# Attention block on one core: plain queries made with dimensions on the partitions, one small query transfer a step, rows of x interleaved

## What is computed

```
xn = _layernorm(x)
c_Q = rms_norm(xn @ Wq_down, q_norm_w)                 # 192 wide
q_nop = (c_Q @ Wq_up)     # 16 heads x 128             plain part of a query
q_pe = rope(c_Q @ Wq_pe)  # 16 heads x 64              rotated part
c_KV = rms_norm(xn @ Wkv_down, kv_norm_w)              # 128 wide
k_nop, v = split(c_KV @ Wkv_up)  # 8 key heads x 128 each
k_pe = rope(rms_norm(xn @ Wk_pe, k_pe_norm_w))         # 64 wide, shared by the heads
scores = ([q_nop, q_pe] . [k_nop, k_pe]) * SCALE, causal mask, softmax -> attn
y = attn @ v ; x + y @ Wo + ternary(xn) @ w_rram.T
```

## Time and profile before

| what | value |
|---|---|
| time, median of 3 runs | 1701.72 us (1698.91 to 1708.31) |
| the profiled execution's own time | 1702.12 us |
| its span, first to last instruction | 1700.3 us |
| PE busy | 1633.8 us (96%), 9612 matmuls |
| DVE / ACT / POOL busy | 77% / 65% / 34% |
| mean DMA rate | 150 GB/s |

### The profile page before, as it was taken

The page is one execution under the profiler, slowest core; times in us unless marked ns, Lnnn a source line. Parts: engine busy times, 40 slices in busy tenths (PEclk is TensorE's granted clock), DMA queues, the critical chain, the costliest instruction groups (busy, mean ns, idle before and its releaser), DMA issues.

```text
span 1700.3 us, 30407 instructions
## 1 busy us (share of the span) xinstructions
PE 1633.8 (96%) x9612; PEld 837.1 (49%) x9612; DVE 1301.6 (77%) x3369; ACT 1104.3 (65%) x2464; POOL 580.3 (34%) x1048
## 2 busy tenths in 40 slices
PE   4789999999999999999999999999999999999999
PEld 3445455544544445545454445554455444555444
DVE  5888878768688687777868787876868868777765
ACT  5877667567576666656666566756756666666663
POOL 3323334333343233433333333433333323333320
PEclk9999999999999999999999999999999999999999
DMA  9467988879979889987969988887987988998886
GB/s 259 97 103 141 150 147 154 147 134 158 152 138 161 145 152 159 166 149 122 161 126 167 170 148 147 154 149 129 161 153 141 159 144 151 162 159 147 147 153 126
DMA packets 914889, 254.58 MB, mean 150 GB/s; under 512 B 901608, under 2 KB 904042, under 8 KB 914410
## 3 DMA queue, kind: packets, MB, share of 16 engines
q1 hardware_dynamic: 904032, 228.98, 80.3%
q10 hardware_dynamic: 9162, 17.37, 3.3%
q0 software_dynamic: 1536, 6.29, 1.1%
HBM read 19.76 MB, written 8.39 MB: 17 GB/s over the span
## 4 chain that ended last, share of the span: by engine, by line
PE 71%; DMA 9%; issue 6%; ACT 5%; DVE 5%; SPq 2%; POOL 2%; ACTq 0%; DVEq 0%; POOLq 0%
DMA FT<-F 6%; PE bank L695 5%; PE bank L693 5%; PE bank L692 5%; PE bank L694 5%; PE bank L795 5%; PE bank L794 5%; PE bank L793 5%; PE bank L737 4%; PE bank L738 4%; PE bank L739 4%; PE bank L705 4%; ACT P L1082 2%; SPq L1848 2%; DVE F L1499 2%
## 5 line engine op out<-in xcount | busy, mean ns | idle before, releaser
L1082 ACT ACTIVATE P<-P,nm 128x256 f32<-128x256 f32 (+15 forms) x512 | 381.7, 746 | 439.6 <-DVE nm L1485 439.6
L1485 DVE CUSTOM_DVE_ANT_0 P<-bank,mask,neg 128x256 f32<-128x256 f32 (+15 forms) x512 | 383.0, 783 | 270.0 <-PE bank L705 261.8
L1719 POOL TENSOR_SCALAR sn<-sm 128x1 f32<-128x1 f32 x512 | 209.0, 409 | 926.1 <-ACT P L1082 918.6
L1077 ACT ACTIVATE F<-P,rc 128x256 f16<-128x256 f32 (+15 forms) x512 | 366.7, 743 | 101.0 <-DVE rc L1493 62.4
L1499 DVE SCALAR_TENSOR_TENSOR F<-P,rc,F 128x256 f16<-128x256 f32 (+15 forms) x512 | 401.6, 796 | 2.7 <-ACT F L1077 2.3
L692 PE MATMUL bank<-K,Q 128*128 128x512 f16 (+7 forms) x760 | 241.7, 319 | 0.8 <-DMA Q<-QS 0.8
L695 PE MATMUL bank<-K,Q 128*128 128x512 f16 (+7 forms) x760 | 241.7, 319 | 0.0
L693 PE MATMUL bank<-K,Q 128*128 128x512 f16 (+7 forms) x760 | 241.7, 319 | 0.0
L694 PE MATMUL bank<-K,Q 128*128 128x512 f16 (+7 forms) x760 | 241.7, 319 | 0.0
L793 PE MATMUL bank<-WO,YH 128*128 128x512 f16 x512 | 194.3, 379 | 4.0 <-DVE YL L1505 3.7
L794 PE MATMUL bank<-WO,YH 128*128 128x512 f16 x512 | 194.0, 379 | 0.0
(11 more groups left out here) (229 smaller groups left out, 2874.8 us busy)
## 6 DMA issues: line engine op xcount, KB each, us to landing
out<-X ACTq DMA_DIRECT2D x31, 256.0 KB, 3.6
X<-in_x ACTq DMA_DIRECT2D x28, 256.0 KB, 3.5
FT<-F SPq DMA_TRANSPOSE x348, 4.4
wo<-in_Wo POOLq DMA_DIRECT2D x4, 1024.0 KB, 7.0
Q<-QS SPq DMA_TRANSPOSE x256, 3.6
V<-CC SPq DMA_DIRECT2D x32, 64.0 KB, 3.0
X<-in_x SPq DMA_DIRECT2D x4, 256.0 KB, 8.4
kv<-in_Wkv_up POOLq DMA_DIRECT2D x1, 1024.0 KB, 12.5
```

Of the source, the lines that this page charges most:

```text
L1077: return e.eng.activation(dst, src, ACT.Copy, scale=scale)
L1082: e.eng.activation(m.P[:, u % 4, 0:w], m.P[:, u % 4, 0:w], ACT.Exp, bias=m.nm[:, u % 8:u % 8 + 1], scale=-1.0, accum_out=m.sm[:, u % 8:u % ...
L1485: e.eng.tensor_tensor_reduce(out=m.P[:, u % 4, 0:w], in0=m.pS[u % 2][:, off:off + w], in1=m.mask[:, end - w:end], scale=m.neg[:, :], scala ...
```

## The change

1. **Rows of x.** `rows` gives a tile's 128 rows in another order: partition 2k + a holds row 64a + k, so the two sides alternate from partition to partition. x is loaded and the output stored in that order; the table for the rotation is loaded likewise, by two transfers. V is brought back to natural order by two transfers with every second partition of CC. K is turned into a new buffer KT, and GpSimd copies it in natural order to its place (`keep_keys`, new semaphore `k_at`).
2. **Plain queries.** `up` now takes slices of WM as weights and C as the moving operand. Its output has the 128 dimensions on the partitions and 128 positions on the columns, one head after another: 4 heads x 5 matmuls of 128 columns. ScalarE and VectorE write high and low parts straight into Q, which has four buffers in place of two.
3. **Rotated part.** Only this is turned: one transfer of 128 positions x 512 columns a step, from QS to QP.
4. **Weights of the score products.** The 128 queries of a side are now every second column (`[:, a::2]`) of two neighbouring heads.
5. **Output of the value products.** The pattern into pY becomes `p (h q a) -> p a h q`: each side writes every second 4-byte word, so that the positions in pY come to lie in the new order.
6. **Half matmuls.** The four 64-row halves of `up` stand between the matmuls of `diagonal_half`.

```
 def rows(dram, t):
     b, i = ORDER[t]
-    return dram[b, i * 128:i * 128 + 128, :]
+    return by_places(dram[b, i * 128:i * 128 + 128, :])
+def by_places(dram):
+    return dram.rearrange("(a k) n -> k a n", a=2)
...
 def query_weights(m, n, h):
     a, g = divmod(h, 2)
-    Q = m.Q[:, n % 2, a, :]
-    return [Q[:, 256 * x + 128 * g:256 * x + 128 * g + 128] for x in range(3)]
+    Q, heads = m.Q[:, n % 4, :, :], slice(2 * g, 2 * g + 2)
+    return [x[:, heads, :].rearrange("p h q -> p (h q)")[:, a::2] for x in (Q[:, 0:4, :], Q[:, 4:8, :], m.QP[:, n % 2, :, :])]
...
     def up(self, n, begun=False):
-        e.eng.matmul(m.pU, hq, W[:, WMA:WMA + 512], start=not begun, stop=False)
-        if not begun:
-            e.eng.matmul(m.pU, lb, W[:, WMB:WMB + 512], start=False, stop=False)
-        e.eng.matmul(m.pU, hq, W[:, WMA + 512:WMA + 1024], start=False, stop=False)
-        e.eng.matmul(m.pU, lq, W[:, WMA:WMA + 512], start=False, stop=False)
-        e.eng.matmul(m.pU, hb, W[:, WMB:WMB + 512], start=False, stop=True).then_inc(s.up, 1)
+        for h in range(4):
+            o, W = m.pU[:, 128 * h:128 * h + 128], m.WM[:, g, 128 * h:]
+            e.eng.matmul(o, W[:, WMA:WMA + 128], hq, start=not begun and h == 0, stop=False)
+            if not begun:
+                e.eng.matmul(o, W[:, WMB:WMB + 128], lb, start=False, stop=False)
+            e.eng.matmul(o, W[:, WMA + 512:WMA + 640], hq, start=False, stop=False)
+            e.eng.matmul(o, W[:, WMA:WMA + 128], lq, start=False, stop=False)
+            op = e.eng.matmul(o, W[:, WMB:WMB + 128], hb, start=False, stop=(h == 3))
+        op.then_inc(s.up, 1)
...
     def weighed(n, j, lo, hi):
-        o = m.pY[n % 2].rearrange("p (h a q) -> p a h q", h=4, a=2)[:, lo // 2:hi // 2]
+        o = m.pY[n % 2].rearrange("p (h q a) -> p a h q", h=4, a=2)[:, lo // 2:hi // 2]
...
+    def keep_keys(self, t):
+        e.wait_ge(s.k_in, 16 * (t + 1))
...
+        e.eng.tensor_copy(m.K[:, :, at:at + 128].rearrange("p c (a k) -> p c a k", a=2),
+                          m.KT.rearrange("p c (k a) -> p c a k", a=2)).then_inc(s.k_at, 1)
...
     def turn_queries(n):
-        e.wait_ge(s.qh, n + 1)
-        e.wait_ge(s.ql, n + 1)
         e.wait_ge(s.ph, n + 1)
         e.wait_ge(s.pl, n + 1)
         if n >= 2:
             e.wait_ge(s.s, 4 * (n - 1))
-        for a in range(2):
-            e.eng.dma_start_transpose(out=m.Q[:, n % 2, a, :].rearrange("p (c q) -> p c q", q=64),
-                                      in_=m.QS[64 * a:64 * a + 64, n % 2, :]).then_inc(s.q_in[a][n % 2], 16)
+        e.eng.dma_start_transpose(out=m.QP[:, n % 2, :, :], in_=m.QS[:, n % 2, :]).then_inc(s.q_in[n % 2], 16)
```

More of the change, by code:

```diff
@@ L225, in __init__ @@
         self.K = own("K", [128, 4, 2048], F16)
+        self.KT = own("KT", [128, 4, 128], F16)
         self.V = own("V", [128, 2 * NT, 2, 128], F16)
@@ L244, in __init__ @@
         self.FT = own("FT", [128, RING * 1024], F16)
-        self.Q = own("Q", [128, 2, 2, 768], F16)
-        self.QS = own("QS", [128, 2, 1536], F16)
+        self.Q = own("Q", [128, 4, 8, 128], F16)
+        self.QP = own("QP", [128, 2, 4, 128], F16)
+        self.QS = own("QS", [128, 2, 512], F16)
         self.R1 = own("R1", [128, 4, 64])
@@ L404, in rotated_parts @@
 def rotated_parts(m, n):
-    flat = m.QS[:, n % 2, 1024:1536]
+    flat = m.QS[:, n % 2, :]
     hi = bass.AP(flat.tensor, flat.offset, [flat.ap[0], [320, 2], [128, 2], [1, 64]])
@@ L481, in up_ready, with up_half @@
             e.wait_ge(s.ql, n)
-    def up_half(self, n):
+    def up_half(self, n, h):
         m, (t, g) = self.m, divmod(n, NG)
         self.up_ready(n)
-        self.e.eng.matmul(m.pU, m.C[64:128, t % 2, 3, :], m.WM[64:128, g, WMB:WMB + 512], start=True, stop=False)
+        at = WMB + 128 * h
+        self.e.eng.matmul(m.pU[:, 128 * h:128 * h + 128], m.WM[64:128, g, at:at + 128], m.C[64:128, t % 2, 3, :],
+                          start=(h == 0), stop=False)
     def up(self, n, begun=False):
@@ L663, in score @@
         qh, ql, qp = query_weights(m, n, h)
-        e.wait_ge(s.q_in[h // 2][n % 2], 16 * (n // 2 + 1))
-        e.wait_ge(s.k_in, 16 * (n // NG + 1))
+        e.wait_ge(s.ql, n + 1)
+        e.wait_ge(s.q_in[n % 2], 16 * (n // 2 + 1))
+        e.wait_ge(s.k_at, n // NG + 1)
         if u >= 2:
@@ L683, in pair @@
         base, K = key_slot(b, 0) * 128, m.K
-        e.wait_ge(s.q_in[p][n % 2], 16 * (n // 2 + 1))
-        e.wait_ge(s.k_in, 16 * (n // NG + 1))
+        e.wait_ge(s.ql, n + 1)
+        e.wait_ge(s.q_in[n % 2], 16 * (n // 2 + 1))
+        e.wait_ge(s.k_at, n // NG + 1)
         for h in (2 * p, 2 * p + 1):
@@ L714, in weigh_ready @@
             e.wait_ge(s.ft_in[z % FSLOTS], 16 * (z // FSLOTS + 1))
-        e.wait_ge(s.v_in, 16 * (n // NG + 1))
+        e.wait_ge(s.v_in, 32 * (n // NG + 1))
         if n >= 2:
@@ L739, in weigh, with diagonal_half @@
         e.eng.matmul(o, vl, hi, start=False, stop=stop).then_inc(s.pv, 1)
-    def diagonal_half(n, first, start=False):
+    def diagonal_half(n, x, start=False):
         o, vh, vl, hi, lo = weighed(n, where(n)[1], 0, 2)
@@ L746, in diagonal_half @@
             weigh_ready(n)
[L747 to L751, removed]
+        v, f = ((vh, hi), (vh, lo), (vl, hi))[x]
+        e.eng.matmul(o, v[0:64], f[0:64], start=start, stop=False)
     def diagonal_rest(n, first, stop=False):
@@ L816, in tensor_attention @@
                 queries.up_pe_half(n + 2 * AHEAD)
-                diagonal_half(n, True, start=True)
+                diagonal_half(n, 0, start=True)
                 diagonal_rest(n, True)
@@ L822, in tensor_attention @@
             if q == 2 and second:
-                queries.up_half(n + 2 * AHEAD)
-                diagonal_half(n, False, not first and done == 0)
+                queries.up_half(n + 2 * AHEAD, 0)
+                diagonal_half(n, 1, not first and done == 0)
+                queries.up_half(n + 2 * AHEAD, 1)
+                queries.up_half(n + 2 * AHEAD, 2)
+                diagonal_half(n, 2)
+                queries.up_half(n + 2 * AHEAD, 3)
                 if not first:
-                    diagonal_half(n, True)
+                    diagonal_half(n, 0)
                     diagonal_rest(n, True)
@@ L941, in queries_hi @@
         e.wait_ge(s.up, n + 1)
[L942 to L945, removed]
+        e.eng.activation(m.Q[:, n % 4, 0:4, :].rearrange("p h q -> p (h q)"), m.pU, ACT.Copy).then_inc(s.qh, 1)
     def rotated_hi(self, n):
@@ L1122, in store_half @@
         at = slice(256 * k, 256 * k + 256)
-        e.eng.dma_start(rows(out, T - 1)[:, at], m.X[:, (T - 1) % XSLOTS, at]).then_inc(s.st_o, 16)
+        e.eng.dma_start(rows(out, T - 1)[:, :, at], m.X[:, (T - 1) % XSLOTS, at]).then_inc(s.st_o, 16)
     def outputs_out(o):
@@ L1302, in queries_lo @@
         e.wait_ge(s.qh, n + 1)
-        e.eng.tensor_tensor(m.QS[:, n % 2, 512:1024], m.pU, m.QS[:, n % 2, 0:512], ALU.subtract).then_inc(s.ql, 1)
+        hi, lo = (m.Q[:, n % 4, 4 * x:4 * x + 4, :].rearrange("p h q -> p (h q)") for x in range(2))
+        e.eng.tensor_tensor(lo, m.pU, hi, ALU.subtract).then_inc(s.ql, 1)
 def vector_prologue(e, m, s, tiles, queries):
@@ L1537, in vector_attention @@
     e.wait_ge(s.sco, 1)
-    e.wait_ge(s.ld_rope, 48)
+    e.wait_ge(s.ld_rope, 64)
     e.wait_ge(s.const, 10)
@@ L1653, in keys @@
         e.eng.tensor_tensor(lo, twice, hi, ALU.subtract).then_inc(s.kl, 1)
+    def keep_keys(self, t):
+        e, m, s = self.e, self.m, self.s
+        b, i = ORDER[t]
+        at = key_slot(b, i) * 128
+        e.wait_ge(s.k_in, 16 * (t + 1))
+        if b:
+            e.wait_ge(s.wom, 16)
+        if b >= 2:
+            e.wait_ge(s.s, 4 * NG * (LAST_OF[b - 2] + 1))
+        e.eng.tensor_copy(m.K[:, :, at:at + 128].rearrange("p c (a k) -> p c a k", a=2),
+                          m.KT.rearrange("p c (k a) -> p c a k", a=2)).then_inc(s.k_at, 1)
 class PoolQueries:
@@ L1697, in gpsimd_prologue @@
     e.eng.tensor_scalar(m.tern[:, :, :], m.fw[:, :, :], -0.2, None, ALU.is_lt).then_inc(s.tern, 1)
-    e.wait_ge(s.v_in, 16)
+    tiles.keep_keys(0)
+    e.wait_ge(s.v_in, 32)
     outputs.load(2)
@@ L1711, in gpsimd_prologue @@
     e.eng.memset(m.mask[:, 0:256], 0.0).then_inc(s.zero, 1)
+    tiles.keep_keys(1)
 def gpsimd_attention(e, m, s, tiles, queries):
@@ L1742, in gpsimd_attention @@
                 tiles.x_lo(t + LEAD)
+            if (g, p) == (3, 1) and t + LEAD - 1 < T:
+                tiles.keep_keys(t + LEAD - 1)
 class SyncTiles:
@@ L1776, in keep @@
             e.wait_ge(s.up, NG * (t - 1))
+            e.wait_ge(s.k_at, t)
         if b:
@@ L1783, in keep @@
             s.c_in, 16)
-        e.eng.dma_start_transpose(out=m.K[:, :, at * 128:at * 128 + 128],
+        e.eng.dma_start_transpose(out=m.KT[:, :, :],
                                   in_=m.CC[:, 1, :, :].rearrange("p a n -> p (a n)")).then_inc(s.k_in, 16)
-        e.eng.dma_start(m.V[:, at, :, :], m.CC[:, 1, :, 0:128]).then_inc(s.v_in, 16)
```

(5 more changed lines are left out.)

19 lines of the change are left out of this document (8 added, 11 removed).

## The result

The changed kernel takes 2043.62 us (median of 4 runs, 2041.72 to 2044.01) against 1701.70 us before: a ratio of 1.200, with a 95% interval of 1.1965 to 1.2036. That is 342 us slower. The forecast of 1699 us was wrong. The rival "lone words in pY", held at 0.38, had forecast 2068 us.

What follows compares the result with a forecast made beforehand. TensorE, busy 96% of the span, was taken to bound the kernel: 1702.1 + 6.6 (query products in pieces) - 10 (lighter transfers) = 1699 us, other terms 0. The range was 1690 to 2080 us, to include lone words.

Steps and rivals of the forecast that it cites:

- lone words in pY: Rival: TensorE must write neighbouring pairs to hold its pace, so every value product takes twice as long; 2068 us, chance 0.38.
- What bounds the kernel: TensorE, busy 96% of the span, is at its wall; changing another engine can bring at most 38 us.
- The output of the value products: Value products writing every second word of pY: taken as 0, the other end being +374 us.
- The pieces: Query products of 512 columns split into four of 128: +6.6 us, range 3.5 to 9.5.
- The halves: Four halves of 128 columns alternating with two of 256: taken as 0, other end +36 us.
- The weights with a step: Score products' weights with a step of two elements: taken as 0; as a rival +13.4 us, 1712 us, chance 0.16.
- The keys: GpSimd's added copy of 128 x 512 a tile, 1.2 us each: hidden, 0; at worst +38 us.
- The transfers: One smaller query transfer a step in place of two shortens TensorE's waits for FT: -10 us, ends 0 and -15.4.
- almost as late: At TensorE's waits for FT: the softmax (ACT, then DVE's F) comes next, limiting the gain to 10 of 15.4 us.

Runs made afterwards that it cites:

- e4: The changed kernel with the value products' output in runs of two neighbouring words on 8-byte borders, the two sides alternating: 1688.61 us.
- e8: The changed kernel with lone words in pY 8 words apart in place of 2: 2042.91 us.
- e11: The changed kernel with two-word runs in pY beginning on odd words, across 8-byte borders, only two heads' values made (252 columns a matmul): 1684.93 us.
- e1: The changed kernel with only the output pattern of the value products put back to runs of 64 words: 1686.45 us, ratio to before 0.990.
- e9: The corrected kernel without GpSimd's copy of the keys, the transfer writing K at once: 1687.36 us, ratio to before 0.9904.
- the corrected kernel: The changed kernel with TensorE writing whole sides (runs of 256 words) into pY and ScalarE's and VectorE's copies interleaving them: 1688.17 to 1688.89 us.

## Why the prediction was wrong, point by point

*What bounds the kernel* was right: TensorE was at its wall at 0.2157 us for 512 columns, and the change in one matmul's pace came through undiminished (+342 us by the distances below, of 357 between the two kernels).

*The output of the value products* is the step that failed. It was put at 0 because the nearest row has hops at full pace, and the other end, +374 us, was held as a rival at 0.38. Measured, the pattern costs 357 us. The nearest row, runs of 64 words, couldn't decide it: e4 shows that runs of two aligned words behave like it, and e8 and e11 that lone words and shifted pairs do not. What the row did hold was the pace itself, 2.37 columns a ns, and the runs show that it is reached only where two columns in turn fill one aligned 8-byte word. The Trainium skill states this in "Advanced Engine Details and Errata", "PSUM Cachelines": lines of 8 bytes, and every two consecutive elements contiguous for best throughput. The runs agree with that sentence to the full factor of two, and with e11 that alignment belongs to it. Its broader sentence, that any non-contiguous pattern slows matmuls, they deny: 0.216 us with a hop every two words. The prediction set both sentences against the trace and saw the broad one denied. It then held against the rival that no row shows a loss at the hops that exist, but those rows bear on the broad sentence alone; on the narrow one there was no row.

*The size of that term.* Distances between starts, summed over the trace of the changed kernel and of e1: the full value products take 565.2 against 290.1 us, +275 (287 predicted); the diagonal ones 73.6 against 42.8, +31 (41); the stretches of halves 100.9 against 64.6, +36 (41). With some 15 us at the last step and at the first matmul behind each lone-word group this makes the 357 us between the two kernels. The first lone-word matmul behind a fast one is followed sooner, L771 0.18 us after L770 rather than 0.21, and what is behind the last one starts later, L509 0.10 us after L506. The rival's estimate was 5% too high.

*The pieces* were right: 0.0562 us a piece in e1, 516 x (4 x 0.0562 - 0.2157) = +4.7 us, within 3.5 to 9.5; 6.6 was taken. The 81 ns of the Trainium skill ("TensorE: Matmul & The Clock Gate", "Back-to-back issue gap") did not show up here. *The halves* were right: the stretch takes 0.31 or 0.32 us in e1 as before. *The weights with a step* cost nothing at 64 columns. *The keys* cost nothing (e9); one copy took 0.61 us, where 1.2 had been estimated.

*The transfers* were right in kind and too small: TensorE's idle time from 62 us on falls from 38.3 to 19.3 us in e1, 19.0 us where 10 were taken. The transposing queue's share fell to 67.3% there; 69% was forecast. The waits for FT fell from 15.4 us to this row, the only one left:

```profile
PE bank L762 <- DMA FT<-F: 0.9, 2, 0.5
```

The softmax behind it was not "almost as late". The changed kernel itself doesn't show any of this, since its slow TensorE hides it.

With these sizes the forecast for everything but pY would have been 1702 + 5 - 19 = 1688 us, which is what the corrected kernel takes; e1 takes 1686.45 us.

## What to carry to other kernels

When a change permutes data, let TensorE write its output in aligned pairs of neighbouring words at least, and put the finer permutation into the copy that leaves PSUM. There it was free, as a read with a hop. Where TensorE is busy for 96% of the span and at its pace, a pattern of its operands that no row shows is the first risk, ahead of every transfer: price it by the pace that it would break. And where a rival costs some twenty times what the change can gain (357 against 17 us), try a single matmul in that pattern before the whole kernel is written for it.

## What the runs showed that was not expected

- TensorE's output goes at one aligned 8-byte word per two columns: 512 columns took 0.216 us in runs of 64 words and in aligned pairs, 0.43 us as lone words 2 or 8 words apart, and 252 columns took 0.213 us in pairs across the border.
- Weights with a step of two 16-bit elements load behind as few as 64 columns (0.03 us a matmul).
- ScalarE's and VectorE's reads of PSUM with a hop at every element cost nothing (579 and 681 ns for 512 columns). Writes of every second 16-bit element cost them 0.14 to 0.15 and 0.05 us.
- Some 1.1 us more a step on the queue that issues the transposing transfers made the kernel 3% slower than before at equal bytes, though that queue waits for 518 us of the run. Part of it came through the clock: eight of TensorE's longer waits were each followed by some us at 0.5, which cost 19 us in all.
